# Low levels of a level-weighted attention summed in 32-column tiles of the array, with a re-sorted order of steps

## What is computed

```python
gc = jnp.cumsum(g, axis=1).transpose(0, 2, 1)
diff = jnp.where(causal, gc[:, :, :, None] - gc[:, :, None, :], -jnp.inf)
decay = jnp.exp(diff)
lvl = fenwick_level_map(T, NL)
lam_ts = jnp.take_along_axis(lam.transpose(0, 2, 1, 3), lvl[None, None], axis=3)
qk = jnp.einsum('btgn,bsgn->bgts', Cm, Bm)
att = qk * decay * lam_ts
y = jnp.einsum('bhts,bshp->bthp', att, v) + D_res
```

## Time and profile before

| | |
|---|---|
| three runs | 2324.88, 2326.39, 2329.33 us |
| median | 2326.39 us |
| the profiled execution | 2335.59 us, span 2333.7 us |
| PE busy | 2126.1 us, 91% of the span |
| DVE, ACT, POOL busy | 74%, 62%, 35% |
| mean granted clock of PE | 0.964 of full speed |

### The profile page before, as it was taken

How to read it: one execution, slowest core, us unless ns; L and a number is a source line. 1 busy time by engine, 2 the same in 40 slices (tenths; PEclk the granted TensorE clock), 3 DMA queues, 4 the chain that set the end, 5 groups by cost and what they waited for, 6 DMA issues and landing times. The chain is left out here.

```text
span 2333.7 us, 47546 instructions
## 1 busy us (share of the span) xinstructions
PE 2126.1 (91%) x16832; PEld 1618.6 (69%) x16832; DVE 1719.7 (74%) x4431; ACT 1454.2 (62%) x3113; POOL 819.1 (35%) x1204
## 2 busy tenths in 40 slices
PE   4879889999999999999999999999999999998866
PEld 2556667777777777776777777777777777676544
DVE  6666878787887878787787878788797878755433
ACT  3555657677675766767575766767576676754332
POOL 5212332434343433424333333434333342424131
PEclk9979999999999999999999999999999999998777
DMA  5020112121202112120211212110211212010110
GB/s 152 4 47 10 38 35 47 35 48 29 43 17 45 41 36 50 35 47 8 44 37 37 48 36 48 36 37 15 45 40 36 50 35 45 15 46 21 31 34 5
DMA packets 185820, 88.01 MB, mean 38 GB/s; under 512 B 118297, under 2 KB 179873, under 8 KB 180417
## 3 DMA queue, kind: packets, MB, share of 16 engines
q1 hardware_dynamic: 185584, 84.97, 15.4%
HBM read 51.12 MB, written 33.55 MB: 36 GB/s over the span
## 5 line engine op out<-in xcount | busy, mean ns | idle before, releaser
L1186 DVE SCALAR_TENSOR_TENSOR work<-psA,c_conv_w,work 128x255 f32<-128x255 f32 (+2 forms) x810 | 329.2, 472 | 15.6 <-ACT work L926 14.7
L1261 DVE TENSOR_REDUCE nmax<-psB 128x2 f32<-128x512 f32 x512 | 315.9, 679 | 27.5 <-PE psB L741 27.3
L609 PE MATMUL psA<-xnT_a,c_w_in 128*128 128x256 f32 x1088 | 309.9, 409 | 27.7 <-ACT X L950 15.9
L1213 DVE TENSOR_TENSOR att<-att,QK 128x1024 f32<-128x1024 f32 x192 | 235.4, 1253 | 85.4 <-ACT att L963 85.2
L845 PE MATMUL psB<-c_w,hid 128*128 128x128 f32 x2048 | 280.2, 282 | 7.3 <-ACT pt L1009 5.9
L845 PEld LDWEIGHTS psB<-c_w,hid 128*128 128x128 f32 x2048 | 257.8, 194 | 41.1 <-issue 19.0
L1009 ACT ACTIVATE pt<-psB 128x512 f32<-128x512 f32 x512 | 264.4, 606 | 33.0 <-PE psB L760 33.0
L833 PE MATMUL psB<-x1T,c_w 128*128 128x256 f32 x1024 | 276.6, 398 | 6.2 <-ACT hid L1051 5.4
L963 ACT ACTIVATE att<-psA 128x512 f32<-128x512 f32 x384 | 204.5, 610 | 109.7 <-PE psA L650 83.0
L1032 ACT ACTIVATE hid<-psB,c_b 128x256 f32<-128x256 f32 x496 | 210.8, 484 | 57.8 <-PE psB L833 53.6
L609 PEld LDWEIGHTS psA<-xnT_a,c_w_in 128*128 128x128 f32 x1088 | 194.6, 201 | 72.5 <-ACT X L950 24.1
(11 more groups left out here) (246 smaller groups left out, 4275.1 us busy)
## 6 DMA issues: line engine op xcount, KB each, us to landing
qk_scr<-qparts SPq DMA_DIRECT2D x128, 192.0 KB, 2.5
q_stack<-qk_scr SPq DMA_DIRECT2D x96, 192.0 KB
k_stack<-qk_scr SPq DMA_DIRECT2D x32, 576.0 KB
lvl_scr<-work SPq DMA_DIRECT2D x32, 192.0 KB, 5.2
low<-lvl_scr SPq DMA_DIRECT2D x256, 1.5 KB
c_w_in<-in_in_wT SPq DMA_DIRECT2D x1, 2176.0 KB, 9.3
x<-in_x SPq DMA_DIRECT2D x16, 128.0 KB, 4.4
c_w<-in_W SPq DMA_DIRECT2D x2, 1024.0 KB
```

The costliest lines, as they stand in the source:

```text
L609: e.matmul(t[:, 0:T], w_in[:, first + j * P:first + (j + 1) * P], xnT_a[:, :], start=True, stop=True).then_inc(filled[b], 1)
L1186: m = e.scalar_tensor_tensor(out=cv[:, back:], in0=t[:, 0:T - back], scalar=conv_w[:, c, tap:tap + 1], in1=cv[:, back:], op0=ALU.mult, op1 ...
L1213: e.tensor_tensor(att[:, :, :], att[:, :, :], bc(QK[:, kq, :], 1, HG), ALU.mult).then_inc(att_done, 1)
L1261: e.tensor_reduce(nmax[:, i, 2 * h2:2 * h2 + 2], t[:, :].rearrange("p (h k) -> p h k", k=T), AX.X, ALU.max).then_inc(drained[b], 1)
```

## The change

Each quarter's low product now writes the 32 partitions of its own keys only (rows r to r+32 of the bank, 32 columns of the array), and the four quarters' matmuls stand one behind the other, after both high matmuls of the tile. The mask of keys in a later quarter, which `low_sel` no longer reaches, becomes three more rows of the high product (`OFF_LATER`), which POOL writes once at the start; the high product has 120 rows instead of 117. `PERIOD` is another permutation of the same steps; its beginning is cut at another place, so that many lags read one higher, which alone moves nothing.

```diff
@@ constants
-OFF_HIGH, OFF_TOP = 3 * H, 3 * H + 3 * NHI * NT
+OFF_LATER = 3 * H
+OFF_HIGH, OFF_TOP = OFF_LATER + NQ - 1, OFF_LATER + NQ - 1 + 3 * NHI * NT
@@ shape_constants
-            low[OFF_MASK + r, q, q * QT + r:] = NEG
+            low[OFF_MASK + r, q, q * QT + r:(q + 1) * QT] = NEG
...
+        for q in range(NQ - 1):
+            hi[OFF_LATER + q, t, (q + 1) * QT:] = NEG
@@ PERIOD
-load_x0.0+0 tail0.5+3 up0.0+3 ep1.0+4 fn0.0+2 relu0.0+3 ocopy1.0+4 es1.1+4 lvl0.0+1 exps1.1+4 down1.6+5 fn0.1+2
+load_x0.0+0 weigh0.5+2 acc1.4+5 exps0.3+3 gated0.1+2 sum0.3+2 gated0.2+2 wexp0.4+2 wexp0.5+2 gates0.3+1 ep0.3+3
...
@@ tensor, weigh
                         for half in range(2):
                             t, b, u = bank(hop, 2 * s + half)
-                            bv = t[:, :].rearrange("p (t h) -> p t h", h=HG)
                             c = half * 64
                             if u:
                                 e.wait_ge(drained[b], u)
-                            m = e.matmul(bv, sel[0:R_HIGH, :], high_buf[0:R_HIGH, c:c + 64, h0:h0 + HG],
-                                         start=True, stop=not diag, skip_group_check=True)
-                            if diag:
-                                for q in (2 * half, 2 * half + 1):
-                                    m = e.matmul(bv[:, q * QT - c:(q + 1) * QT - c, :], low_sel[0:R_LOW, q, :],
-                                                 low_buf[0:R_LOW, tt * P + q * QT:tt * P + (q + 1) * QT, h0:h0 + HG],
-                                                 start=False, stop=(q % 2 == 1), skip_group_check=True)
-                            m.then_inc(filled[b], 1)
+                            m = e.matmul(t[:, :].rearrange("p (t h) -> p t h", h=HG), sel[0:R_HIGH, :],
+                                         high_buf[0:R_HIGH, c:c + 64, h0:h0 + HG], start=True, stop=not diag,
+                                         skip_group_check=True)
+                            if not diag:
+                                m.then_inc(filled[b], 1)
+                        if diag:
+                            for q in range(NQ):
+                                t, b, u = bank(hop, 2 * s + q // 2)
+                                r, c = q * QT, (q % 2) * QT
+                                m = e.matmul(t[:, :].rearrange("p (t h) -> p t h", h=HG)[r:r + QT, c:c + QT, :],
+                                             low_sel[0:R_LOW, q, r:r + QT],
+                                             low_buf[0:R_LOW, tt * P + r:tt * P + r + QT, h0:h0 + HG],
+                                             start=False, stop=True, skip_group_check=True)
+                                if q % 2:
+                                    m.then_inc(filled[b], 1)
@@ gpsimd, gates0.0 of the first sequence
+                        later = slice(OFF_LATER, OFF_LATER + NQ - 1)
+                        e.tensor_copy(high_buf[later, 0:(NQ - 1) * QT, :].rearrange("a (q t) h -> a q (t h)", t=QT),
+                                      bc(ident[later, later], 2, QT * H)).then_inc(*own.step())
+                        e.wait_ge(*own.now())
```

More of the change, by code:

```diff
@@ L129 @@
-tail0.2+2 up1.7+4 smax1.2+3 ssq0.0+1 ssq0.1+1 relu1.7+4 ssq0.2+1 ssq0.3+1 tail0.3+2 rowmax1.2+3 smax1.3+3
-gates0.4+0 outp0.0+1 tail0.4+2 rowmax1.3+3 maxt1.0+3 outp0.1+1 gates0.5+0 gates0.6+0 place0.0+0 v1.0+3 es1.0+3
-exps1.0+3 conv0.0+0 outp0.2+1
+load_x0.0+0 weigh0.5+2 acc1.4+5 exps0.3+3 gated0.1+2 sum0.3+2 gated0.2+2 wexp0.4+2 wexp0.5+2 gates0.3+1 ep0.3+3
+prod0.4+2 own0.4+2 own0.5+2 prod0.5+2 gated0.3+2 sum0.4+2 ocopy0.3+3 weigh0.6+2 relu1.5+5 wexp0.6+2 gated0.4+2
+own0.6+2 up1.6+5 relu1.6+5 prod0.6+2 tail0.0+3 sum0.5+2 gated0.5+2 weigh0.7+2 wexp0.7+2 down1.5+5 gates0.4+1
@@ new lines @@
+own0.7+2 acc1.5+5 prod0.7+2 sum0.6+2 smax1.0+4 sum0.7+2 gated0.6+2 rowmax1.0+4 tail0.1+3 smax1.1+4 gated0.7+2
+rowmax1.1+4 up1.7+5 tail0.2+3 smax1.2+4 ssq0.0+2 ssq0.1+2 relu1.7+5 tail0.3+3 ssq0.2+2 ssq0.3+2 rowmax1.2+4
+smax1.3+4 outp0.0+2 tail0.4+3 rowmax1.3+4 gates0.5+1 maxt1.0+4 gates0.6+1 v1.0+4 tail0.5+3 outp0.1+2 tail0.6+3
+place0.0+1 outp0.2+2 es1.0+4 conv0.0+1 exps1.0+4 fn0.0+2 up0.0+3 experts0.0+3 ep1.0+4 relu0.0+3 experts0.1+3
+es1.1+4 conv0.1+1 ocopy1.0+4 exps1.1+4 down1.6+5 tap0.0+1 fn0.1+2 ep1.1+4 lvl0.0+1 lvl0.1+1 ocopy1.1+4 q0.0+2
@@ new lines @@
+acc1.6+5 es1.2+4 conv0.2+1 down0.0+3 up0.1+3 taps0.0+1 down1.7+5 exps1.2+4 tap0.1+1 acc0.0+3 acc1.7+5 ep1.2+4
+tap0.2+1 taps0.1+1 relu0.1+3 es1.3+4 down0.1+3 ocopy1.2+4 exps1.3+4 up0.2+3 up0.3+3 acc0.1+3 relu0.2+3 silu0.0+1
+conv0.3+1 relu0.3+3 taps0.2+1 q0.1+2 down0.2+3 tap0.3+1 acc0.2+3 up0.4+3 relu0.4+3 up0.5+3 zgate0.0+1 down0.3+3
+down0.4+3 silu0.1+1 xt0.0+1 experts1.2+5 conv0.4+1 zact0.0+1 silu0.2+1 relu0.5+3 gates0.0+0 taps0.3+1 tap0.4+1
+acc0.3+3 xt0.1+1 up0.6+3 silu0.3+1 acc0.4+3 bcp0.0+1 up0.7+3 xcopy0.0+1 conv0.5+1 taps0.4+1 relu0.6+3 tap0.5+1
@@ new lines @@
+down0.5+3 down0.6+3 experts1.3+5 xt0.2+1 relu0.7+3 down0.7+3 zgate0.1+1 taps0.5+1 conv0.6+1 acc0.5+3 acc0.6+3
+ep1.3+4 xcopy0.1+1 silu0.4+1 xt0.3+1 acc0.7+3 experts0.2+3 xcopy0.2+1 tap0.6+1 zact0.1+1 ocopy1.3+4 taps0.6+1
+experts0.3+3 silu0.5+1 tail1.0+4 conv0.7+1 xcopy0.3+1 tap0.7+1 tail1.1+4 taps0.7+1 mix1.0+3 xt0.4+1 tail1.2+4
+v0.0+2 zgate0.2+1 silu0.6+1 silu0.7+1 smax0.0+2 zgate0.3+1 zact0.2+1 tail1.3+4 xcopy0.4+1 xt0.5+1 mix1.1+3
+zact0.3+1 smax0.1+2 xt0.6+1 conv0.8+1 xcopy0.5+1 lvl0.2+1 rowmax0.0+2 tail1.4+4 smax0.2+2 rowmax0.1+2
@@ new lines @@
+rowmax0.2+2 xcopy0.6+1 tap0.8+1 lvl0.3+1 mix1.2+3 mix1.3+3 tail1.5+4 tail1.6+4 mix1.4+3 lvl0.4+1 lvl0.5+1
+mix1.5+3 qk0.0+1 taps0.8+1 up1.0+4 up1.1+4 relu1.0+4 lvl0.6+1 relu1.1+4 mix1.6+3 experts1.0+4 mix1.7+3 mix1.8+3
+mix1.9+3 zgate0.4+1 mix1.10+3 down1.0+4 qkc0.0+1 experts1.1+4 up1.2+4 acc1.0+4 relu1.2+4 zact0.4+1 zgate0.5+1
+coef0.0+1 smax0.3+2 lvl0.7+1 zact0.5+1 own0.0+1 rowmax0.3+2 zgate0.6+1 silu0.8+1 mix1.11+3 zgate0.7+1 zact0.6+1
+zact0.7+1 down1.1+4 maxt0.0+2 weigh0.0+1 down1.2+4 acc1.1+4 wexp0.0+1 mix1.12+3 weigh0.1+1 wexp0.1+1 gates0.1+0
@@ L132 @@
+up1.3+4 acc1.2+4 weigh0.2+1 es0.0+2 prod0.0+1 sum0.0+1 xt0.7+1 relu1.3+4 fn1.0+3 exps0.0+2 prod0.1+1 wexp0.2+1
+up1.4+4 fn1.1+3 own0.1+1 ep0.0+2 relu1.4+4 ocopy0.0+2 q1.0+3 weigh0.3+1 gated0.0+1 prod0.2+1 wexp0.3+1 es0.1+2
+sum0.1+1 exps0.1+2 own0.2+1 q1.1+3 down1.3+4 ep0.1+2 xcopy0.7+1 es0.2+2 acc1.3+4 ocopy0.1+2 prod0.3+1 exps0.2+2
+gates0.2+0 down1.4+4 ep0.2+2 es0.3+2 sum0.2+1 weigh0.4+1 up1.5+4 own0.3+1 ocopy0.2+2
 """
```

## The result

The changed kernel is slower: 2362.06 us (median of 4 runs, 2358.41 to 2364.06) beside 2325.64 for the kernel before, a ratio of 1.0153 [1.0134, 1.0171]. The forecast was 2315.6.

A forecast was written before the change was run, and what follows sets the result against it. PE was taken to set the pace, busy 127.6 of a 132.6 us period. Tiles saving 0.09 us in each of 120 units made 10.8 us, all else 0: 2326.4 to 2315.6 us, range 2298 to 2326.

The forecast's parts named there:

- rival "slower": Each quartet's four weight loads show on PE: unit 1.12 us against 0.88, 29 us more, 2355 us; chance 0.05.
- "Four low ones 0.44 us" to 0.35: A `weigh` unit's four low products on PE as 32-column tiles: 0.09 us less per unit, 10.8 us per launch.
- Way in: PE's border from a full-width matmul into 32-column tiles: 0.10 us per quartet.
- way out: PE's border from the tiles back to a full-width group: taken as 0.14 us per quartet, 0.16 at the other end.
- rival 2: Tile borders drain PE in full, 0.16 us each: quartet 0.43 instead of 0.44, 2325 us, no change; chance 0.06.
- "Work taken from PE should shorten the period by itself": PE has no wait from 1087 to 1129, all of `weigh`; savings there count in full for 120 of 128 units.
- clock of 1.00 in the middle: PE's granted clock in the period read, 2.4 GHz; no lower level assumed.
- own sign: PE's clock below 1.00 in the middle of the span would prove the whole sum wrong.
- "Late first bank: cost nothing": A unit's first bank fills at about 0.66 instead of 0.44 us; cover before `sum` hides the 0.22 us delay.
- "POOL's extra copy: nothing": POOL's one copy at the start takes 2.7 us, hidden because POOL then idles 6.65 us before dependent work.
- The order, counted as 0 with -21 as its better end: Permuted steps: gain and loss of one size, counted 0, ends -21 to +6.5 us per launch.
- rival 1: New order gives back PE's waits, 0.43 to 1.39 us more per sequence: 2309 to 2295 us; chance 0.22.

The follow-up runs named there:

- experiment 2: Kernel before, its step list kept, with only the tiles and mask rows added: 2332.21 us, ratio 1.0013.
- experiment 6: Kernel before with both high products of a diagonal tile first, then four full-width low ones, no tiles: 2335.24 us, ratio 1.0008.
- experiment 5: Kernel before (full-width low products) with the new step list, where `mix1.12` no longer asks for the silu tables: 2316.12 us, ratio 0.9926.
- experiment 1: Changed kernel, same list, but `mix1.12` no longer asks for the silu tables, so the extra table loads go: 2325.81 us, ratio 0.9987.

## Why the prediction was wrong

**What made it slower was no term of the sum.** I read the new list for what PE, DVE and SP do, and noted that the steps are permuted; I didn't ask which steps `order()` inserts on its own. ACT's row count and its table loads in the new order would have shown 28 more instructions. The loads alone put +1.66% on the kernel (1.0153 less 0.9987), some of it by way of the clock that fell behind the new wait. The rival "slower" that I did write, exposed weight loads, didn't happen.

**"Four low ones 0.44 us" to 0.35: the quartet is cheaper than forecast, its surroundings dearer.** Way in 0.10, as forecast; a quartet to the next group 0.22, so a way out of 0.11 instead of 0.14, and a unit of 0.76 instead of 0.79. The 0.38 us at which rival 2 would have begun was not reached (0.30 to 0.33). What failed is "a way out", read as one number: when an f32 group follows, its own length grows by 0.10 us more. The earlier trace rows held it, as the length 1.16 of the `down` group behind `sum`; behind a bf16 product of full width the same group has 1.05 (1089.49, experiment 2). I read the distance and not the length. A unit so gains 0.12 us ahead of bf16 and about 0.02 ahead of the f32 groups of `up` and `down`.

**"Work taken from PE should shorten the period by itself" failed.** The timeline showed no wait between 1087 and 1129, but no wait isn't play. In the kernel before, the group ahead of `fn1.1` takes 1.08 us (1093.69 to 1094.77) where such a group behind tiles streams in 0.99 (experiment 2), so PE already stood there for 0.09 us. The brackets can't show that: they count from the end of a group, here 1093.69 + 1.16 = 1094.85, which lies behind the next start. The forecast's clock of 1.00 in the middle was read in one period that has it. Before, five of the twelve periods have a stretch at the lower level and are 1.1 us longer, and seven with the change. By the forecast's own sign that puts its sum in doubt: it had no term for the clock.

**"Late first bank: cost nothing" failed** for the same reason. I checked the cover of `sum`, 1.2 us, which held. The next step of DVE behind `prod`, `src`, had none (experiment 6). A second cost wasn't on the list: in the new list both high products first leave PE with nothing to do while a bank is still busy, 0.48 us a sequence in units 4, 6 and 7 together with the dearer f32 groups behind them (experiment 5).

**"POOL's extra copy: nothing" failed by 2.1 us.** I had its length right (2.75 against 2.7) and looked at POOL's own dependants, not at DVE, which works against POOL at that time.

**The order, counted as 0 with -21 as its better end, is worth -17 us** (experiment 5, ratio 0.9926). The forecast's rival 1 was right in size, but by luck: the three waits shrank from 2.1 to 0.17 us and 1.7 us returned at other steps. A distance gained 0.55 us, of which 0.46 is the lower clock that no longer follows those waits and 0.09 the waits themselves. Half of the gain lies ahead of sequence 3, where I had looked at nothing; how much of it is the clock no run separates.

**The sum as measured**, as ratios to before: list -0.74%, tiles with mask rows and copy +0.61% in this list, loads +1.66%: together +1.53%. On full-width products in this list the loads cost +1.44% (1.0070 less 0.9926), and 1.68 us of distance at the upper level (134.22 less 132.54) where they cost 1.50 with the tiles. The two differences point opposite ways, and the first is within the intervals of its four ratios; whether tiles and loads add up isn't shown.

**Open.** Of the 10.5 us between the spans of experiments 1 and 5 (2323.9 less 2313.4), 2.2 lie ahead of the first unit (the copy), 2.1 from there to sequence 3, 3.3 in the twelve distances and 3.0 behind the last first unit; the second and the last weren't taken apart. What makes the clock fall in some sequences and not in others isn't shown. That the extra 0.10 us of an f32 group is a weight load that isn't brought forward past the tiles was not tried.
